# Small-head attention in groups of two heads at the first pack, and at the last pack of the first attention

## What is computed

```python
scores = jnp.einsum('bhqd,bhkd->bhqk', q, k) * scale      # 16 heads of 8 channels
attn = jax.nn.softmax(scores, axis=-1)
out = jnp.einsum('bhqk,bhkd->bhqd', attn, v)
...
scores = jnp.where(causal, scores, jnp.float32(-1e+30))   # in the second of the two
...
x = _layernorm(x + _L0_attn_ref(...), axis=-1)
x = _layernorm(x + _L0_ffn_ref(...), axis=-1)
x = _layernorm(x + _L1_attn_ref(...), axis=-1)
x = _layernorm(x + _L1_ffn_ref(...), axis=-1)
```

## Time and profile before

| | |
|---|---|
| runs | 2236.6, 2239.74, 2245.05 us; median 2239.74 |
| profiled execution | 2239.87 us, its span 2238.1 us |
| mean granted TensorE clock | 0.898 of full |
| busy | TensorE matmul 84%, VectorE 72%, ScalarE 61%, GpSimd 13% |
| first attention, first reduction to last copy of the output bank (L620, L585) | 82.7 to 746.6 us |
| second attention, the same | 1670.5 to 2097.4 us |

### The profile page before, as it was taken

One profiled execution on the slowest core, in us unless ns is written; L12 is line 12 of the kernel. 1 busy time (PEld: TensorE's weight loads), 2 busy tenths in 40 slices (PEclk: granted clock), 3 DMA queues, 4 the chain that ended last, 5 costly groups with the idle time before them and its releaser, 6 DMA issues. The chain is left out here.

```text
span 2238.1 us, 40233 instructions
## 1 busy us (share of the span) xinstructions
PE 1884.7 (84%) x16064; PEld 928.5 (41%) x16064; DVE 1600.8 (72%) x2303; ACT 1364.8 (61%) x2538; POOL 301.3 (13%) x463
## 2 busy tenths in 40 slices
PE   7679999999999579568888999999476999999675
PEld 2112222222222268534566777777211232334375
DVE  4799999999994443435765677776559988886334
ACT  3259989989899433234544566665342887877321
POOL 2000000000000151413321211111200000000023
PEclk7579999999999779879999999999666999999777
DMA  5000000000000169500000000000100000000074
GB/s 156 1 1 7 4 6 5 7 4 4 6 4 6 41 203 305 162 2 0 1 1 1 1 1 1 1 1 1 49 1 1 5 7 4 7 9 9 11 256 164
DMA packets 51355, 81.34 MB, mean 36 GB/s; under 512 B 7520, under 2 KB 36192, under 8 KB 51040
## 3 DMA queue, kind: packets, MB, share of 16 engines
q1 hardware_dynamic: 46000, 70.30, 9.9%
q0 software_dynamic: 3072, 6.30, 0.9%
q10 hardware_dynamic: 2096, 2.17, 0.3%
HBM read 62.49 MB, written 11.67 MB: 33 GB/s over the span
## 5 line engine op out<-in xcount | busy, mean ns | idle before, releaser
L596 ACT ACTIVATE a0a_probs<-psum 128x512 f32<-128x512 f32 x1024 | 553.8, 596 | 108.1 <-PE psum L536 101.1
L620 DVE TENSOR_REDUCE a0a_mx<-psum 128x2 f32<-128x1024 f32 x512 | 583.2, 1207 | 9.2 <-PE psum L516 9.0
L516 PE MATMUL psum<-a_KS,a_QS 48*128 48x512 bf16 (+3 forms) x1664 | 332.8, 393 | 78.4 <-DVE a0a_mx L620 42.7
L596 ACT ACTIVATE a1a_probs<-psum 128x512 f32<-128x512 f32 (+3 forms) x640 | 304.5, 533 | 117.5 <-PE psum L536 77.9
L620 DVE TENSOR_REDUCE a1a_mx<-psum 128x2 f32<-128x1024 f32 (+2 forms) x320 | 323.6, 1059 | 52.0 <-PE psum L516 29.2
L536 PE MATMUL psum<-a_QS,a_KS 51*128 51x512 bf16 (+3 forms) x1664 | 336.2, 380 | 11.0 <-ACT a1a_probs L596 4.0
L559 PE MATMUL psum<-a0a_probs,a_V 128*16 128x256 f32 x4096 | 326.5, 390 | 8.0 <-ACT a0a_OD L585 5.5
L1584 PE MATMUL psum<-b_VW,b_ST 128*128 128x129 f32 x2176 | 257.0, 280 | 16.2 <-DVE X L1695 16.2
L1584 PEld LDWEIGHTS psum<-b_VW,b_ST 128*128 128x128 f32 x2176 | 253.9, 197 | 17.4 <-DVE X L1695 17.4
L1564 PE MATMUL psum<-b_GT,AT 128*128 128x512 f32 (+3 forms) x640 | 245.2, 537 | 16.9 <-ACT b_ST L1623 16.9
L536 PEld LDWEIGHTS psum<-a_QS,a_KS 51*128 51x128 bf16 x1664 | 87.2, 93 | 368.3 <-ACT a0a_probs L596 196.2
(11 more groups left out here) (221 smaller groups left out, 1731.2 us busy)
## 6 DMA issues: line engine op xcount, KB each, us to landing
e_W<-in_l_experts SPq DMA_DIRECT2D x46, 576.0 KB, 5.3
e_W<-in_l_experts SPq DMA_DIRECT2D x22, 768.0 KB, 5.0
yg<-e_yout SPq DMA_DIRECT2D x14, 256.0 KB, 5.9
xg<-zeros SPq DMA_DIRECT2D x2, 1472.0 KB, 9.4
a_cs<-in_rope ACTq DMA_DIRECT2D x4, 512.0 KB, 9.0
a_cs<-in_rope SPq DMA_DIRECT2D x1, 2048.0 KB, 7.9
e_xin<-xg SPq DMA_DIRECT2D x2, 896.0 KB, 8.2
AT<-in_xT SPq DMA_DIRECT2D x4, 256.0 KB, 6.0
```

The costliest lines, as they stand in the source:

```text
L516: mm = pe.matmul(ps[:, 2 * slot + half, 0:width], QS[rows, 2 * p + i, q_cols(qb, qt * P, P)], KS[rows, 2 * p + i, c * BLK:c * BLK + width] ...
L596: act.activation(probs[:, e % P_SLOTS, c:BLK], ps[:, S_BANK + e % S_SLOTS, c:BLK], ACT.Exp, scale=scale).then_inc(exp_done, 1)
L620: dve.tensor_reduce(mx[:, pk % 2, qt, 2 * i:2 * i + 2, c], banks, AX.X, ALU.max).then_inc(max_done, 1)
```

## The change

`small_head_attention` and `Plan` take a list `split` of (block, pack) pairs. A pack named there becomes two packs of two heads, unit (0,) and unit (1,), with 16 scores items each without a mask, a maximum, a turn and a set of steps of its own. The first attention gets ((0, 0), (3, 3)), its first and its last pack, the causal one ((3, 0),), its first. A step of such a pack has one score pair, two exponentials and two products in each half. The assumed step time is now per head. All semaphore counts follow the number of heads of a pack.

```diff
-    def __init__(self, causal, order):
+    def __init__(self, causal, order, split):
...
-        self.packs = [(qb, p) for qb in order for p in range(NPACK)]
-        self.steps = [(P_, kt) for P_, (qb, p) in enumerate(self.packs) for kt in range(self.key_tiles(qb))]
+        self.packs, self.block_first = [], []
+        for qb in order:
+            self.block_first.append(len(self.packs))
+            for p in range(NPACK):
+                self.packs += [(qb, p, (0,)), (qb, p, (1,))] if (qb, p) in split else [(qb, p, (0, 1))]
...
+        self.steps = [(P_, kt) for P_, pack in enumerate(self.packs) for kt in range(self.key_tiles(pack[0]))]
+        self.exp0 = [0]
+        for pk, kt in self.steps:
+            self.exp0.append(self.exp0[-1] + len(self.heads(pk)))
...
-            begin.append(begin[-1] + HPP * (0.11 + 0.00085 * (BLK - self.first_col(s))))
+            begin.append(begin[-1] + len(self.heads(self.steps[s][0])) * (0.11 + 0.00085 * (BLK - self.first_col(s))))
...
+    def heads(self, pk):
+        return [2 * i + half for i in self.packs[pk][2] for half in range(2)]
...
-        for i in range(2):
+        for i in units:
             for qt in range(TPB):
...
-                    for j in range(HPP):
+                    for n, j in enumerate(plan.heads(pk)):
                         r = HALF * (j % 2) + SHIFT0
                         sp.dma_start(QS[r:r + TERMS, 2 * p + j // 2, q_cols(qb, 0, BLK)],
-                                     mrow[TERMS * j:TERMS * (j + 1), pk % 2, :]).then_inc(shift_in[p], 16)
+                                     mrow[TERMS * n:TERMS * (n + 1), pk % 2, :]).then_inc(shift_in[kind(pk)], 16)
...
-                    for j in range(HPP):
+                    for j in plan.heads(pk):
                         h = (HPP * p + j) * HD
                         for dst, r in ((num, 32 * j), (den, 32 * j + HD)):
...
-                        pe.wait_ge(exp_done, HPP * (s + 1))
+                        pe.wait_ge(exp_done, plan.exp0[s + 1])
...
-                    for j in range(HPP):
-                        e = HPP * s + j
+                    for n, j in enumerate(plan.heads(pk)):
+                        e = plan.exp0[s] + n
                         mm = pe.matmul(ps[32 * j:32 * j + 2 * HD, AV_BANK, a:b], V[:, kt, HPP * p + j, :],
...
-                    row = plan.rows[s]
+                    row, units = plan.rows[s], plan.packs[plan.steps[s][0]][2]
                     for half in range(2):
-                        score(s, half)
+                        if half < len(units):
+                            score(s, units[half])
...
-                small_head_attention(core, "a0a", KS, QS, V, AT, False, forward)
+                small_head_attention(core, "a0a", KS, QS, V, AT, False, forward, ((0, 0), (NB - 1, NPACK - 1)))
...
-                small_head_attention(core, "a1a", KS, QS, V, AT, True, forward[::-1])
+                small_head_attention(core, "a1a", KS, QS, V, AT, True, [3, 2, 1, 0], ((3, 0),))
```

More of the change, by code:

```diff
@@ L348, in __init__, with head_cols, uses, last_on @@
             count += item[0] == "scores"
+    def heads(self, pk):
+        return [2 * i + half for i in self.packs[pk][2] for half in range(2)]
+    def head_cols(self, pk):
+        heads = self.heads(pk)
+        return slice(heads[0], heads[-1] + 1)
+    def uses(self, pk):
+        p, units = self.packs[pk][1:]
+        return sum(1 for q in range(pk + 1) if self.packs[q][1:] == (p, units))
+    def last_on(self, pk):
+        p, units = self.packs[pk][1:]
+        return [q for q in range(pk) if self.packs[q][1] == p and self.block[q] == self.block[pk] - 1
+                and set(self.packs[q][2]) & set(units)]
     def key_tiles(self, qb):
@@ L385, in on_diagonal, with small_head_attention @@
         return self.causal and kt >= TPB * self.packs[pk][0]
-def small_head_attention(core, tag, KS, QS, V, OT, causal, order):
+def small_head_attention(core, tag, KS, QS, V, OT, causal, order, split):
     nc, ps = core.nc, core.psum
     scale = float(HD) ** -0.5
-    plan = Plan(causal, order)
+    plan = Plan(causal, order, split)
     NS, NPK = len(plan.steps), len(plan.packs)
     H2 = BLK // 2
-    TR = HPP * TERMS
+    kinds = sorted({pack[1:] for pack in plan.packs})
+    kind = lambda pk: kinds.index(plan.packs[pk][1:])
     def q_cols(qb, a, n):
@@ L461, in _ @@
                     (shift, gather)[what](pk)
-                for p in range(NPACK):
-                    sp.wait_ge(shift_in[p], 16 * HPP * NB)
-                    sp.wait_ge(gathered[p], 16 * 2 * HPP * NB)
+                for pk in range(plan.block_first[NB - 2], NPK):
+                    wait_shift(sp, pk)
+                    wait_gathered(sp, pk)
             @block.gpsimd
@@ L580, in od_copy @@
                 def od_copy(pk):
-                    p, k = pk % NPACK, pk // NPACK
+                    p, heads = plan.packs[pk][1], plan.heads(pk)
                     act.wait_ge(av_done, plan.first[pk + 1])
-                    if k:
-                        act.wait_ge(gathered[p], 16 * 2 * HPP * k)
-                    act.activation(OD[:, p, :], ps[:, AV_BANK, :], ACT.Copy).then_inc(od_done, 1)
+                    for q in plan.last_on(pk):
+                        wait_gathered(act, q)
+                    rows = slice(32 * heads[0], 32 * heads[-1] + 32)
+                    act.activation(OD[rows, p, :], ps[rows, AV_BANK, :], ACT.Copy).then_inc(od_done, 1)
                 for s in range(NS):
@@ L589, in _ @@
                     c = plan.first_col(s)
-                    for j in range(HPP):
-                        e = HPP * s + j
+                    for n in range(len(plan.heads(pk))):
+                        e = plan.exp0[s] + n
                         act.wait_ge(s_ready, e + 1)
-                        if j == 0 and s >= 2:
+                        if n == 0 and s >= 2:
                             act.wait_ge(av_done, s - 1)
```

61 lines of the change are left out of this document (33 added, 28 removed).

## The result

The changed kernel takes 2261.92 us (median of 5 runs, 2256.73 to 2262.82) and the kernel before 2240.16 beside it (5 runs, 2236.60 to 2245.05): a ratio of 1.0093, with a 95% interval of 1.0077 to 1.0108. It is slower by 21.8 us. The forecast was 2253.0, between 2243 and 2263. The profiled executions have spans of 2260.1 and 2238.1 us.

The account below looks back on a forecast made before the run. VectorE's reductions were taken to set the pace, ScalarE only where none are left. 2239.87 + 3.4 (start) - 4.3 + 14.1 (first attention's end) - 2.7 (gather) + 2.6 (second attention) = 2253.0 us, range 2243 to 2263.

Parts of the forecast that it names:

- new step 43: Start of the first attention: the plan state of old step 27 is reached there, 3.4 us later (0 to +6).
- The sixteen steps from there to new step 251: End of first attention: 64 exponentials with 17 items, paced by ScalarE, take 34.6 us, not 38.9: -4.3.
- The last 84 exponentials: End of first attention: to the last product they take 59.5 us instead of 45.4, +14.1.
- a narrow product costs as much as a wide one: Two-head steps: a product half takes as long as for four heads, so a step without items takes 1.31 us.
- The gather: End of first attention: four transfers in place of eight, issued 0.67 us apart, save 2.7 us.
- an earlier start of ScalarE is worth nothing by itself: First attention: first exponential at 107.5 us instead of 126.91, without gain, as VectorE sets the pace.
- The second attention: Its split first pack: old step 26's place comes at 1784.7 us instead of 1782.13, +2.6 (-2 to +6).
- 2.5 more for the low clock: Second attention's narrow steps: the low clock adds 2.5 us to VectorE's 66.8.
- 1.5 less for that lead: Second attention's narrow steps: items issued that VectorE has yet to reduce take 1.5 us off.
- Narrow products cost half: Rival: narrow steps without items take ScalarE's 1.06 us, so the kernel takes 2245; chance 0.15.
- The short tail is real: Rival, end of first attention: VectorE holds its pace into the last pack, last product 8.9 us earlier, 2228; chance 0.08.
- Narrow steps are slower still: Rival: waits of 0.25 us a step, or low clock at the end, add some 7 us: 2260; chance 0.17.

Follow-up runs that it names:

- first0: The changed kernel with only the first pack of the first attention split: 2243.66 us, ratio 1.0016 to the kernel before.
- first1: The changed kernel with only the first pack of the second attention split: 2246.79 us, ratio 1.0031 to the kernel before.
- after_again: The changed kernel measured once more in another series, no edit: 2257.59 us, ratio 1.0072 to the kernel before.
- the single splits: Three runs of the changed kernel, each with one of its three splits left in: 3.6, 6.9 and 6.9 us slower than the kernel before.
- the last series: Kernel before with reductions ordered 6.5 us ahead, not 10, in the first attention; alone, and with later last turn and faster last gather: ratios 0.9981, 0.9943.
- early_tail: The changed kernel with reductions of the first attention's last two narrow packs due 8 and 11 steps earlier: 2255.25 us, ratio 1.0066 to the kernel before.
- half_product: The changed kernel without the second product half in the first attention's last two narrow packs: one run of 2250.57 us.

## Why the prediction was right in sign and short in size

**The first attention** went by its steps. At new step 43 the forecast was +3.4 and the profile has +4.1 (+3.9 at new step 235; *first0* +3.5). The sixteen steps from there to new step 251 were to take 34.6 us and took 35.1: -3.8 in place of -4.3. The last 84 exponentials were to need 59.5 us to the last product and needed 57.8: +12.4 in place of +14.1. Together +12.4 where +13.2 stood; the three parts miss by +0.5, +0.5 and -1.7 and cancel in part. The step on which most of it rests, that a narrow product costs as much as a wide one, is shown twice: 1.30 us per step against the 1.31 worked out from the rows, and 1.05 once the second half is taken away. The gather was to save 2.7; its last issue comes 759.15 - 755.45 = 3.70 us after the start of the last product in place of 751.91 - 745.50 = 6.41, and that is 2.7.

**The start.** The view "an earlier start of ScalarE is worth nothing by itself" held: 19.6 us earlier, and 3.5 to 3.9 later at new step 235. VectorE sets the pace from the first instruction, and *first0* has nothing else to show for its split.

**The second attention is the step that failed**: "63 x 1.03 + 2 x 0.94 = 66.8 us of VectorE from 1694.7 on ..., with 2.5 more for the low clock and 1.5 less for that lead", +2.6 in all. The work was right: VectorE is busy for 38.08 + 29.48 = 67.6 us in the 32 narrow steps. Missing was what it waits for. The steps take 71.2 us in place of 68.2. VectorE's timeline of the changed kernel:

```profile
1707.68 5.42 DVE L653 TENSOR_REDUCE a1a_mx<-psum 128x2 f32<-128x1024 f32 x5 [2.09 <-PE psum L546]
...
1760.93 0.42 DVE L653 TENSOR_REDUCE a1a_mx<-psum 128x2 f32<-128x256 f32 x1 [0.24 <-PE psum L522]
1761.80 2.36 DVE L653 TENSOR_REDUCE a1a_mx<-psum 128x2 f32<-128x1024 f32 x2 [0.44 <-PE psum L546]
```

VectorE has run dry 2.09 us before the first of these reductions, so there is no lead of 1.5 to take off. At the lower clock (1.2 GHz, a granted clock of 0.50 up to 1716.0) it then idles 1.6, where 2.5 + 0.4 was allowed; and at full clock it idles 2.0 more, in gaps of up to 0.44 as in the last two rows, where the forecast had none: by its terms TensorE's 1.96 for two items lies under VectorE's mean of 2 x 1.03 = 2.06. That mean hides that reductions as short as 0.42 stand beside full ones, and that a masked item has matmuls of its own for the mask (L522). Some 1.3 of the 2.0 stand directly before or behind a reduction of 0.68 us or less, the rest between full ones; this reading of the gaps was not tried in a run. With 0.8 more of work the sum is 0.8 - 1.3 + 1.5 + 2.0 = 3.0, all by which the narrow steps are longer than forecast. Of the other 2.7 of the miss, 1.7 lie in the ten wide steps (23.9 us for 22.2) and 1.2 behind them, less 0.2 ahead of the first exponential. Without chance the split costs +5.5 (*first1*; 432.7 - 426.8 = +5.9 in *after_again*) where +2.6 stood, and the range for it, -2 to +6, held it.

**The rest is chance of an execution, not the change.** Put together from the single splits the change is +12.4 - 2.7 + 5.5 = +15.2 us, against +13.1 forecast, and *after_again* measured 16. The first series measured 21.8. Its profile has +5.8 between the attentions beside the gather (the distance was 922.2 to 926.4 in the other profiles, the last series aside, 927.0 here), 2.8 more in the second attention, +0.7 behind it, and -2.4 at the start. What makes the distance longer was not tried. That the first series still lay in the range (2261.92 under an upper end of 2263) is luck: the working stands for 13.1 us, near the 15 to 16 that come back, and not for the 21.8.

**The rivals.** *Narrow products cost half* fell with the 1.04 us of eight matmuls; its 1.05 us step appears only where the half is left out. *The short tail is real* fell: the last reduction comes 637.2 us after the first, not 614, and *early_tail*, where it does come at 616.8, is only 1.6 us shorter. At new step 235, 148 exponentials stand in the queue, some 79 us of ScalarE at 0.53 each, whatever VectorE does, and narrow steps make more of them: the last output copy comes 35.1 + 58.8 = 93.9 us after that step, and 92.8 in *early_tail* (674.7 - 581.9). *Narrow steps are slower still* did not hold: at full clock they take 1.30 us, and the low clock did not fall on the last 35 us (a granted clock of 1.00). In the second attention the low clock cost VectorE less than allowed, 1.6 us for 2.9.

## What to carry to other kernels

To split a group so that another engine starts earlier wins nothing if a third engine sets the pace from the first instruction on; count the work that stands before the next common state on the pacing engine, and the gain at the start is gone. Where several small operations lie beside each other in the array, a smaller group keeps the price per step and loses the concurrency, so a shorter last group costs more than the backlog it was to shorten. What helped at the end was to take waits out of the queue that has the backlog: the last row two steps later, and the transfers that the next instruction needs sent first and on two queues.

## What the runs showed of the hardware beyond that

Eight small transfers from one tile to another, issued on one queue 0.67 us apart, hold the reciprocal for 7.4 us; with the four that it needs sent first and on two queues it is 4.4, though ScalarE's queue takes 2.19 us for two issues where SP's takes 1.29. I had put this saving at 4 us.

TensorE's granted clock falls to half for short stretches in the middle of dense work. The busy time of the changed kernel around one of them, 0.72 of full speed over 6 us:

```profile
1780.00:1786.00 6.00, 5.50 (x48) 1.18 (x51) 3.50 (x3) 4.52 (x9) 0.00 (x0) 0.72 0.06 11
```

In the ten wide steps behind the narrow ones of the second attention it lies within the stretch, and they take 23.9 us (so it is in *early_tail*); in *first1*, *after_again* and *half_product* it does not, and they take 22.5. Where one falls differs from run to run and is worth about 1.4 us, so a part of one profile can't be compared with the same part of another more closely than that. The distance from the start of the program to the first reduction differs between executions of kernels that are the same up to there by up to 4.3 us (80.2 to 84.5).
